# Attention inside a fused layer: one product of queries and keys instead of two, and probabilities turned by DMA

## The chip, the cores and the metric

One Trainium2 chip, one core of it. The metric is the device time of one execution in microseconds (us); three runs of the kernel before gave 1651.43 to 1651.74 us, median 1651.48.

## The reference, cut to what matters

```python
xn = layernorm(x)                                   # x: 1 x 2048 x 512
q = xn @ Wq                                         # 16 heads of 32
k, v = split(xn @ Wkv, 2)                           # 4 key/value heads of 32
scores = q @ k.T / sqrt(32) + tril(idx_s - idx_t) * slope[head]
attn = softmax(where(s <= t, scores, -inf), axis=-1)
x = x + (attn @ v) @ Wo + bo + mlp(xn)              # mlp: 512 -> 4096 -> 512, 4-bit weights, gated GELU
```

The score of query t and key s exists only for s <= t. The kernel needs, for each query, the greatest score (to shift the exponent), the exponentials, their sum and their product with the values.

## The kernel before, in words

Everything has fp32 accuracy: an operand is split in a high and a low fp16 part, and three products (high x high, high x low, low x high) make one. Queries and keys are used as fp32.

The main loop has 16 iterations. Iteration i does head i of the attention and one sixteenth of the MLP (256 of its 4096 columns, all 2048 tokens). It is cut into 48 slots (`SLOTS`, L59). In each slot TensorE issues six MLP matmuls of 512 columns in two halves (`mlp(s, 0)`, `mlp(s, 1)`, L1427 and L1434), and round them the attention's work for that slot: 288 MLP matmuls in an iteration. The order on each engine is written out by the tables of a plan (`FIRST_PLAN` for head 0, `EVEN_PLAN` after it, L126 and L129): which block goes in which slot. Each engine walks the slots by itself, in order, and waits on semaphores.

The attention multiplies queries and keys twice:

- `maximum` (L1318) puts 128 queries on partitions and up to 512 keys in the columns (40 blocks of a head, 17,408 columns). VectorE reduces each block to a maximum (`reduce`, L1622: TENSOR_REDUCE for full blocks, a masked reduction for the 16 on the diagonal, each followed by a read of its accumulator). Four small reductions make a high and a low part of the negated maximum of 512 queries (`negate_max`, L1640), `turn_max` (L1352) turns them on TensorE and ScalarE copies them as two more rows into the query operand (`max_rows`, L1510). This runs about half a head ahead.
- `score` (L1365) puts 128 keys on partitions and up to 512 queries in the columns (36 blocks, 17,408 columns), with the negated maximum added by those two rows. VectorE adds the mask on the diagonal (`causal`, L1613, 16 additions). ScalarE takes exponentials (`exp`, L1493) and rounds them to fp16 (`prob_hi`, L1504); GpSimd makes the low part (`prob_lo`, L1777). Keys already lie on partitions, so the fp16 probabilities are the moving operand of the value products as they are.

`values` (L1391) takes up to 8 blocks at a time, six times a head. Each block gives five products with 32 weight columns, which go to four groups of 32 columns of the array in turn: three value products and two with a column of ones, which make the row sums. `o_copy` (L1518) copies both results, and SyncE's queue gathers them: 12 DMAs of values (`gather_o`, L1218), 8 of row sums, then `load_sums`, the reciprocals (`row_sums`, L273) and their spreading.

SyncE's queue (L1147 to L1273) issues every DMA of the loop in program order, with waits between: queries of the next head in four pieces of four DMAs (`load_q`), keys (`load_k`, each head, two buffers), packed weights, and the six crossbar transposes of the decoded weights (`turn_rows`, L381: high and low rows, 128 x 1024 fp16 each, for three matrices).

## Time and profile before

| | us |
|---|---|
| median of the three runs | 1651.48 |
| the profiled execution: its own time | 1653.03 |
| the profiled execution: its span | 1651.0 |
| one head in the steady part (16 in all) | 92.3 |
| before the main loop / after its last values | about 113 / about 70 |

```profile
PE 1606.0 (97%) x9953; PEld 808.8 (49%) x9953; DVE 1210.7 (73%) x2688; ACT 1059.2 (64%) x1740; POOL 1025.1 (62%) x853
PEclk9989999999999999999999999999999999999999
```

PE is TensorE, PEld its weight loads, DVE VectorE, ACT ScalarE, POOL GpSimd, SPq the queue in which SyncE issues DMAs. The first line has busy time and share of the span; the second the clock granted to TensorE in 40 equal slices, in tenths of full speed. Matmuls are pipelined, so their listed durations overlap; the distance between their starts is what they cost.

### The profile page before, as it was taken

To read this page: it belongs to the slowest core of one execution; us is meant where nothing else is said; L and a number is where in the kernel's file an instruction comes from. 1 tells how busy PE (TensorE), PEld (TensorE's weight loads), DVE (VectorE), ACT (ScalarE), POOL (GpSimd) and SP (SyncE) were. 2 spreads that over 40 slices of the span, in tenths; PEclk is the share of its full clock that TensorE was granted. 3 is DMA by queue.
4 is the path that set the end of the run, shared out by engine and by line. 5 is a ranking of instruction groups with operands and counts; after the bars stand their busy time and mean duration, and the time that the engine had idled before them with its cause. 6 is when DMAs were issued, how large, how long until landed. Compare 5 with 4: busy or idle time off the path is not lost.

```text
span 1651.0 us, 30625 instructions
## 1 busy us (share of the span) xinstructions
PE 1606.0 (97%) x9953; PEld 808.8 (49%) x9953; DVE 1210.7 (73%) x2688; ACT 1059.2 (64%) x1740; POOL 1025.1 (62%) x853
## 2 busy tenths in 40 slices
PE   5979999999999999999999999999999999999998
PEld 4754444444444444444444444454544444444443
DVE  7757877777777777776777777776777777776666
ACT  3326677676767766676767767675767667676650
POOL 3215667576767757576767757576766767575550
PEclk9989999999999999999999999999999999999999
DMA  7872232223122132223222231223132231322135
GB/s 218 226 178 74 43 83 47 70 53 79 31 72 67 45 82 49 70 51 79 38 70 62 48 85 43 74 47 79 43 73 54 53 79 43 77 49 72 43 107 190
DMA packets 203956, 125.75 MB, mean 76 GB/s; under 512 B 156128, under 2 KB 173416, under 8 KB 202104
## 3 DMA queue, kind: packets, MB, share of 16 engines
q1 hardware_dynamic: 199480, 118.16, 29.1%
q10 hardware_dynamic: 4320, 5.64, 1.0%
q8 instruction: 82, 1.34, 0.3%
q14 instruction: 74, 0.61, 0.1%
HBM read 63.31 MB, written 22.42 MB: 52 GB/s over the span
## 4 chain that ended last, share of the span: by engine, by line
PE 84%; DVE 5%; issue 2%; DMA 1%; ACT 1%; POOL 0%; SPq 0%; POOLq 0%; DVEq 0%; ACTq 0%
PE up_ps L1314 20%; PE gate_ps L1314 19%; PE down_ps L1292 18%; PE max_ps L1333 8%; PE o_ps L1385 8%; PE score_ps L1376 4%; PE turn_ps L1376 3%; PE l_ps L1385 2%; DVE prod L1603 1%; DVE acc L1579 1%; PE turn_ps L1361 1%; DVE score_ps L1618 0%; DMA wo_tops<-sc 0%; DVE mxp L1637 0%; DMA l_parts<-lraw 0%
## 5 line engine op out<-in xcount | busy, mean ns | idle before, releaser
L1781 POOL TENSOR_TENSOR plo<-p,phi 128x512 f16<-128x512 f32 (+1 forms) x576 | 664.9, 1160 | 263.1 <-ACT phi L1508 259.0
L1508 ACT ACTIVATE phi<-p 128x512 f16<-128x512 f32 (+1 forms) x576 | 348.7, 605 | 16.3
L1637 DVE TENSOR_REDUCE mxp<-max_ps 128x1 f32<-128x512 f32 x373 | 256.5, 688 | 126.2 <-PE max_ps L1333 125.4
L1789 POOL TENSOR_TENSOR il<-prod,ih 128x512 f16<-128x512 f32 x128 | 156.6, 1223 | 236.1 <-DVE ih L1611 236.1
L1501 ACT ACTIVATE p<-score_ps,pshift 128x512 f32<-128x512 f32 (+1 forms) x321 | 207.9, 648 | 147.4 <-PE score_ps L1376 67.9
L1333 PE MATMUL max_ps<-kst,qst 128*128 128x512 f32 (+2 forms) x610 | 253.9, 416 | 6.7 <-DVE mxp L1637 2.8
L1501 ACT ACTIVATE p<-turn_ps,pshift 128x512 f32<-128x512 f32 (+1 forms) x255 | 170.7, 669 | 105.7 <-DVE turn_ps L1618 55.8
L1633 DVE CUSTOM_DVE_ANT_0 max_ps<-max_ps,mask_row 128x512 f32<-128x512 f32 (+1 forms) x237 | 116.6, 492 | 121.7 <-PE max_ps L1333 120.3
L1314 PE MATMUL gate_ps<-xh,wh 128*128 128x512 f16 x512 | 198.0, 387 | 0.0
L1314 PE MATMUL up_ps<-xh,wh 128*128 128x512 f16 x512 | 197.5, 386 | 0.0
L1292 PE MATMUL down_ps<-wh,ih 128*128 128x512 f16 x506 | 194.9, 385 | 0.0
L1314 PE MATMUL gate_ps<-xh,wl 128*128 128x512 f16 x512 | 194.8, 380 | 0.0
L1314 PE MATMUL gate_ps<-xl,wh 128*128 128x512 f16 x512 | 194.8, 380 | 0.0
L1314 PE MATMUL up_ps<-xh,wl 128*128 128x512 f16 x512 | 194.0, 379 | 0.0
L1314 PE MATMUL up_ps<-xl,wh 128*128 128x512 f16 x512 | 194.0, 379 | 0.0
L1292 PE MATMUL down_ps<-wl,ih 128*128 128x512 f16 x506 | 191.8, 379 | 0.0
L1292 PE MATMUL down_ps<-wh,il 128*128 128x512 f16 x506 | 191.8, 379 | 0.0
L1579 DVE TENSOR_TENSOR acc<-down_ps,acc 128x512 f32<-128x512 f32 x237 | 162.4, 685 | 29.4 <-PE down_ps L1292 25.9
L1376 PE MATMUL score_ps<-qst,kst 128*128 128x512 f32 (+2 forms) x355 | 178.5, 518 | 5.6 <-ACT qst L1516 2.9
L1385 PE MATMUL o_ps<-phi,vst 128*32 128x512 f16 (+3 forms) x1744 | 164.4, 348 | 0.0
L1376 PE MATMUL turn_ps<-qst,kst 128*128 128x512 f32 (+3 forms) x285 | 146.5, 531 | 0.0
L1333 PEld LDWEIGHTS max_ps<-kst,qst 128*128 128x128 f32 x610 | 115.6, 189 | 58.9 <-DVE mxp L1637 20.9
(305 smaller groups left out, 2747.4 us busy)
## 6 DMA issues: line engine op xcount, KB each, us to landing
qst<-q_parts SPq DMA_DIRECT2D x192, 64.0 KB
o<-oraw SPq DMA_DIRECT2D x192, 64.0 KB, 2.0
kst<-k_parts SPq DMA_DIRECT2D x45, 256.0 KB, 4.6
q_parts<-o SPq DMA_DIRECT2D x24, 256.0 KB, 3.3
raw<-L_ffn_gate_W_packed_dram SPq DMA_DIRECT2D x16, 256.0 KB, 3.0
raw<-n_L_ffn_up_W_packed_dram SPq DMA_DIRECT2D x16, 256.0 KB, 3.2
raw<-L_ffn_down_W_packed_dram SPq DMA_DIRECT2D x32, 128.0 KB, 3.4
rb<-l_recips SPq DMA_DIRECT2D x16, 256.0 KB
```

The costliest lines, as they stand in the source:

```text
L1292: mm = nc.tensor.matmul(dst[:], lhs, rhs, start=(q == 0), stop=(q == 5))
L1314: mm = nc.tensor.matmul(dst[:], lhs, rhs, start=(q == 0), stop=(q == 11))
L1333: mm = nc.tensor.matmul(bank[:, 0:cols], qst[:, c, t * P:(t + 1) * P], kst[h % 2][:, m * CH:m * CH + cols], start=True, stop=True)
L1376: mm = nc.tensor.matmul(bank[:, col:col + width], kst[par][:, j * P:(j + 1) * P], qst[:, c, tok:CH], start=True, stop=True, skip_group_che ...
L1385: mm = nc.tensor.matmul(bank[g * HD:(g + 1) * HD, tok:CH], vst[:, j, of * HD:(of + 1) * HD], src[n % PP][:, col:col + CH - tok], start=sta ...
L1501: nc.scalar.activation(p32[n % PR][:, 0:cols], bank[:, 0:cols], ACT.Exp, bias=pshift[:, 0:1]).then_inc(exp_done, 1)
L1508: nc.scalar.activation(phi[n % PP][:, 0:cols], p32[n % PR][:, 0:cols], ACT.Copy).then_inc(phi_done, 1)
L1579: nc.vector.tensor_tensor(acc[:, n % NT, :], bank[:], before, ALU.add).then_inc(acc_done, 1)
L1633: nc.vector.tensor_tensor_reduce(bank[:, 0:cols], bank[:, 0:cols], mask_row[:, CH - cols:CH], 1.0, -3e38, ALU.add, ALU.max, mxp[c % 2][:, ...
L1637: nc.vector.tensor_reduce(mxp[c % 2][:, t, m:m + 1], bank[:, 0:cols], AX.X, ALU.max).then_inc(red_done, 1)
L1781: nc.gpsimd.tensor_tensor(plo[n % PP][:, 0:cols], p32[n % PR][:, 0:cols], phi[n % PP][:, 0:cols], ALU.subtract).then_inc(plo_done, 1)
L1789: nc.gpsimd.tensor_tensor(il[w % 2][:, a, :], prod[a][:], ih[w % 2][:, a, :], ALU.subtract).then_inc(il_done, 1)
```

## The change

Queries and keys are multiplied once, with 128 queries on partitions. VectorE takes each block's maximum as before and then makes the shift of one tile of 128 queries by itself, with queries on partitions, so that ScalarE can take the exponential from the same PSUM block with the shift as its per-partition bias. The scores' second product, the turning of the maxima, the mask additions and the two extra rows go. The PSUM banks become a ring of four for these blocks.

ScalarE's exponential also gives the sum of its row (`accum_out`), one for each of the 40 blocks; the products with ones go, and the gathering of their results. The reciprocals are turned on VectorE in 32 x 32 pieces and stored by four small DMAs.

The probabilities now have queries on partitions, and the value products need keys there. So each part (`PARTS`: a tile of 128 queries and up to 1024 keys; 24 in a head, 136 blocks of 128 x 128) is rounded to fp16 in one ScalarE copy and one GpSimd subtraction, and both results are turned by a crossbar transpose DMA each, issued by SyncE: 48 more in a head. Two buffers for each half (`PH = 2`) stand before the transposes; behind them is a ring of room for 42 blocks. A value product covers 256 queries (two tiles) for one block of keys: 193 products of 256 columns and 24 of 128 in a head, in eight calls.

The work of a head starts six slots before its iteration (`LEAD`), so six slots without MLP work stand ahead of the first one. One plan serves all heads. Keys are loaded every fourth head only, and the order on SyncE's queue is written by slots too.

```diff
+BLOCKS = [(TPC * c + i, m) for c in range(NCH) for i in range(TPC) for m in range(c + 1)]
+PARTS = [(t, a) for t in range(NT) for a in range(t // (2 * TPC) + 1)]
+RING = 42
+LEAD = 6
+TILE_START = tuple(range(4)) + (4, 6, 8, 10) + (12, 16, 19, 23) + (26, 31, 36, 41)
+EXP_LAG = ((1,), (1, 1), (1, 1, 2), (1, 1, 2, 3))
+PART_LAG = ((2,), (2,), (2, 3), (2, 3))
+LOW_LAG, VALUES_LAG = 2, 6
+    for n, (t, m) in enumerate(BLOCKS):
+        last = TILE_START[t] + t // TPC
+        put(tables.block_at, TILE_START[t] + m, n)
+        put(tables.exp_at, last + EXP_LAG[t // TPC][m], n)
+    for p, (t, a) in enumerate(PARTS):
+        at = TILE_START[t] + t // TPC + PART_LAG[t // TPC][a]
+        put(tables.part_at, at, p)
+        put(tables.low_at, at + LOW_LAG, p)
+        if p in LAST_PART:
+            put(tables.values_at, at + VALUES_LAG, t // 2)
...
+LOAD_Q_AT = {2: 0, 9: 1, 21: 2, 40: 3}
+GATHER_AT = {1: 3, 7: 0, 15: 1, 30: 2}
...
+        PR, PH = 3, 2
+        s_ring = (s0_ps, s1_ps, s2_ps, s3_ps)
...
             def _(sp):
+                def turn(h, p, done, rows, dst, turned):
+                    t, a = PARTS[p]
+                    n, count = h * NPART + p, min(t + 1 - 2 * TPC * a, 2 * TPC)
+                    sp.wait_ge(done, n + 1 if done is phi_done else after(n + 1))
...
+                    sp.dma_start_transpose(dst[:, at:at + count, :], rows[n % PH][:, 0:count * P]).then_inc(turned[n % PH], 16)
+                def body(i, par, slots):
+                    for s in slots:
+                        for h, p in items(PLAN.low_at, i, s):
+                            turn(h, p, plo_done, plo, ptl, lo_turned)
+                        for h, p in items(PLAN.part_at, i, s):
+                            turn(h, p, phi_done, phi, pth, hi_turned)
...
             def _(pe):
+                    def block(h, n):
...
+                        if g >= len(s_ring):
+                            pe.wait_ge(exp_done, after(g + 1 - len(s_ring)))
+                        cols = columns(t, m)
+                        nc.tensor.matmul(s_ring[n % len(s_ring)][:, 0:cols], qst[:, c, i4 * P:(i4 + 1) * P],
+                                         kst[:, m * CH:m * CH + cols], start=True, stop=True).then_inc(block_done, 1)
+                    def values(h, u):
...
+                        for n in (last - 1, last):
+                            pe.wait_ge(hi_turned[n % PH], 16 * (n // PH + 1))
+                            pe.wait_ge(lo_turned[n % PH], 16 * (n // PH + 1))
+                        for j in range(2 * u + 2):
+                            both = j <= 2 * u
+                            for src, of in ((pth, 0), (pth, 1), (ptl, 0)):
+                                rows = src[:, at + j:at + j + step + 1:step, :] if both else src[:, at + step + j, :]
+                                todo.append((vst[:, j, of * HD:(of + 1) * HD], rows, 0 if both else P))
...
             def _(act):
+                    def exp(h, n):
...
+                        act.wait_ge(shift_done, h * NT + t + 1)
+                        if p >= PR:
+                            act.wait_ge(plo_done, after(p + 1 - PR))
+                        nc.scalar.activation(p32[p % PR][:, at:at + cols], s_ring[n % len(s_ring)][:, 0:cols], ACT.Exp,
+                                             bias=shift[t % len(shift)][:, 0:1], accum_out=lacc[h % 2][:, t, m:m + 1]
                                              ).then_inc(exp_done, 1)
+                    def part_hi(h, p):
...
+                        if n >= PH:
+                            act.wait_ge(hi_turned[n % PH], 16 * (n // PH))
+                            act.wait_ge(plo_done, after(n + 1 - PH))
+                        nc.scalar.activation(phi[n % PH][:, 0:cols], p32[n % PR][:, 0:cols], ACT.Copy).then_inc(phi_done, 1)
...
             def _(dve):
+                    def negate(h, n):
...
+                        dve.wait_ge(red_done, h * NBLK + n + 1)
+                        if c:
+                            nc.vector.tensor_reduce(top, mxp[t % 2][:, 0:c + 1], AX.X, ALU.max).then_inc(best_done, 1)
+                        nc.vector.tensor_scalar(shift[t % len(shift)][:], top, -1.0, PSHIFT, ALU.mult, ALU.add
+                                                ).then_inc(shift_done, 1)
...
             def _(pool):
+                    def part_lo(h, p):
...
+                        if n >= PH:
+                            pool.wait_ge(lo_turned[n % PH], 16 * (n // PH))
+                        nc.gpsimd.tensor_tensor(plo[n % PH][:, 0:cols], p32[n % PR][:, 0:cols], phi[n % PH][:, 0:cols],
+                                                ALU.subtract).then_inc(plo_done, 1)
```

## Rows read from the trace of the kernel before

**Rows 1.** Windows, two steady heads: length, busy us and instructions, PEclk, DMA share, GB/s

```profile
816.90:909.20 92.30, 92.20 (x591) 45.15 (x595) 68.26 (x155) 63.61 (x105) 62.43 (x52) 1.00 0.26 65
909.20:1001.50 92.30, 92.21 (x592) 45.18 (x593) 68.21 (x155) 63.60 (x105) 62.42 (x52) 1.00 0.26 60
```

**Rows 2.** Chain that ended last, the same value batch of two heads: start, us

```profile
909.23 1.84 PE o_ps L1385 x32
...
1001.55 1.84 PE o_ps L1385 x32
```

**Rows 3.** Timeline of PE: one fp32 block between MLP matmuls: start us, us

```profile
847.99 0.38 PE L1314 MATMUL up_ps<-xl,wh 128*128 128x512 f16 x1
848.02 0.58 PE L1333 MATMUL max_ps<-kst,qst 128*128 128x512 f32 x1
848.45 0.39 PE L1314 MATMUL up_ps<-xh,wh 128*128 128x512 f16 x1
848.67 0.38 PE L1314 MATMUL up_ps<-xh,wl 128*128 128x512 f16 x1
```

**Rows 4.** Timeline of PE: into a value batch and out of it

```profile
841.64 0.38 PE L1314 MATMUL gate_ps<-xl,wh 128*128 128x512 f16 x1
841.95 0.39 PE L1385 MATMUL o_ps<-phi,vst 128*32 128x512 f16 x2
...
843.91 0.38 PE L1385 MATMUL o_ps<-phi,vst 128*32 128x512 f16 x1
844.22 0.39 PE L1314 MATMUL gate_ps<-xh,wh 128*128 128x512 f16 x1
```

**Rows 5.** Timeline of PE: narrow products in the smallest batch

```profile
826.40 0.22 PE L1385 MATMUL o_ps<-phi,vst 128*32 128x128 f16 x2
826.46 0.28 PE L1385 MATMUL o_ps<-phi,vst 128*32 128x256 f16 x2
...
826.56 0.38 PE L1385 MATMUL l_ps<-plo,vst 128*32 128x512 f16 x1
```

**Rows 6.** Groups by form, DVE: busy us, mean ns of one, idle before

```profile
L1618 DVE TENSOR_TENSOR score_ps<-score_ps,mask_st 128x128 f32<-128x128 f32 x151 | 41.2, 293 | 39.9 <-PE score_ps L1376 39.5
L1651 DVE TENSOR_REDUCE mxc<-nmx 128x4 f32<-128x4 f32 x64 | 10.1, 158 | 0.0
L1633 DVE DVE_READ_ACCUMULATOR2_ANT mxp<- 128x1 f32 x256 | 36.1, 141 | 0.0
```

**Rows 7.** Groups by form, ACT and POOL

```profile
L1501 ACT ACTIVATE p<-score_ps,pshift 128x512 f32<-128x512 f32 x272 | 184.8, 679 | 121.9 <-PE score_ps L1376 67.9 <-issue 37.0 <-DVE score_ps L1618 16.2
L1508 ACT ACTIVATE phi<-p 128x512 f16<-128x512 f32 x512 | 322.1, 629 | 14.3
L375 ACT ACTIVATE raw<-wf 128x1024 f16<-128x1024 f32 x48 | 50.5, 1053 | 16.7 <-DVE wf L368 16.6
L1781 POOL TENSOR_TENSOR plo<-p,phi 128x512 f16<-128x512 f32 x512 | 616.3, 1208 | 256.9 <-ACT phi L1508 252.7
L379 POOL TENSOR_TENSOR o<-wf,raw 128x1024 f16<-128x1024 f32 x45 | 98.7, 2193 | 0.0
```

**Rows 8.** Line 385 on SyncE's queue: issue in ns min/median/max, first and last start

```profile
L385 SPq DMA_TRANSPOSE wh<-raw x48: 1232/1268/2557, 97.5 to 1482.8; - x48
```

**Rows 9.** Timeline of SyncE's queue: plain issues back to back

```profile
731.97 1.23 SPq L1161 DMA_DIRECT2D qst<-q_parts  x3
...
734.35 1.79 SPq L1231 DMA_DIRECT2D o<-oraw  x3
736.25 0.61 SPq L292 DMA_DIRECT2D rb<-l_recips  x1
```

**Rows 10.** DMA issues of the page's kind: count, median us from issue to landing

```profile
wh<-raw SPq DMA_TRANSPOSE x48, 3.1
```

**Rows 11.** Windows of 1 us behind the transpose issued at 818.05 us

```profile
819.00:820.00 1.00, 1.00 (x10) 0.60 (x6) 0.00 (x0) 0.00 (x0) 1.00 (x2) 1.00 0.83 145
820.00:821.00 1.00, 1.00 (x7) 0.50 (x6) 0.69 (x3) 0.56 (x2) 1.00 (x2) 1.00 0.60 117
```

More of the change, by code:

```diff
@@ L41 @@
 AUG = 8
-NB = 2
 XS = 2.0 ** 4
@@ L1365, in score @@
-                    def score(n):
-                        c, tiles, _ = BLOCKS[n]
-                        for (ahead, turned), at in plan.turn_after.items():
-                            if at == n and ahead == 0:
-                                pe.wait_ge(brow_done, after(i * NCH + turned + 1))
-                        if n == 0 and i:
-                            pe.wait_ge(brow_done, after(i * NCH + 2))
-                        bank = wait_score_bank(("score", n))
-                        for j, col, tok in tiles:
-                            width = CH - tok
-                            mm = nc.tensor.matmul(bank[:, col:col + width], kst[par][:, j * P:(j + 1) * P],
-                                                  qst[:, c, tok:CH], start=True, stop=True,
-                                                  skip_group_check=True)
-                        mm.then_inc(score_done, 1)
@@ L1673, in body @@
                             inner(n)
-                        if maxima:
-                            negate_max(*maxima[0])
+                        for h, block in blocks:
+                            negate(h, block)
                         if last[0] == "up" and last[3]:
```

773 lines of the change are left out of this document (325 added, 448 removed).

## The prediction

> **What bounds the kernel now.** I read the windows of steady heads first. In a head of 92.3 us TensorE is busy for 92.2 at a granted clock of 1.00 (its upper level, 2.4 GHz), VectorE for 68.3, ScalarE for 63.6 and GpSimd for 62.4, with a DMA share of 0.26 [rows 1]. The chain of waits says the same: it runs through TensorE, and the same value batch comes 92.3 us later in the next head [rows 2]. So TensorE's stream bounds, and the other engines have 24 to 30 us of slack in a head. Since listed matmul durations overlap, I price TensorE by distances between starts. The profiled execution took 1653.0 us, 1.5 above the median of the runs shown; the sum is made against it.
>
> **TensorE, per head.** An MLP matmul is followed by the next after 0.22 us; with one fp32 block of 512 columns between them it takes 0.46 [rows 3], so a block costs 0.245 us. (1) The second product of queries and keys goes: 17,408 columns are 34 such blocks, 8.3 us. (2) Four turnings of maxima go, 2,048 columns at the same price: 1.0 us. (3) Value products. In a big batch 36 products start in the 1.96 us from 841.95 to 843.91, so one of 512 columns costs 0.0545, because four column groups run side by side; entering and leaving the batch costs 0.31 instead of 0.22, twice 0.1 [rows 4]. Before: 5 x 34 + 3 = 173 products of 512, 9.4 us, and six batches, 1.2: 10.6. After: 193 of 256 and 24 of 128 columns are 205 of 256; at half of 0.0545 that is 5.6, and eight batches, 1.6: 7.2. Narrow products keep that pace: after the 128-column ones at 826.40 the 256-column ones start 0.06 later, and the next round 0.10 after these [rows 5]. That saves 3.4. The sum is 12.7 us, so TensorE alone would allow a head of 79.6.
>
> The Trainium skill speaks against (3). "TensorE: Matmul & The Clock Gate", section "Back-to-back issue gap", gives about 81 ns per matmul for streams of weight load and matmul at N=128, however little each computes. By that the 217 products would cost 17.6 us and TensorE would need 90. The trace's column groups start four in about 0.1 us and disagree, but its narrow stretch is short; this is a rival below.
>
> **VectorE.** Sixteen mask additions of 0.293 go (4.7 us), and sixteen small reductions of 0.158 (2.5); 28 small ones come (12 reductions and 16 shifts, 4.4) [rows 6]. 68.3 becomes 65.5, of 80: it still has room, but its slack falls from 24 us to 14.
>
> **ScalarE.** 40 exponentials in place of 36 of the same columns: a copy of 512 columns takes 0.629 and one of 1024 takes 1.053, so the fixed part is 0.2 and four more cost 0.8. Copies to fp16 fall from 36 to 24: -2.4. Four copies of row sums and four of turned maxima go, at 0.6 each: -4.8 [rows 7]. The row sum of each exponential is not in this trace. Its bounds are 0 and, if it is a read like VectorE's accumulator, 0.141 each, twice that if ScalarE is slower: 0 to 11 us; I take the row, 5.6 [rows 6]. 63.6 becomes 62.8. **GpSimd** does the same columns in fewer, wider pieces: 512 take 1.208 and 1024 take 2.193, fixed part 0.22, so 12 fewer save 2.7 and one more addition costs 1.2 [rows 7]: 60.9. Neither bounds, but GpSimd works wholly in the chain copy, subtraction, low transpose, values.
>
> **SyncE's queue**, the resource that the page's first part doesn't list. A 128 x 1024 transpose occupies it for 1.23 to 1.27 us [rows 8], a plain DMA of 32 partitions 0.41 to 0.6, and one that spreads 256 KB 0.61 [rows 9]; about 0.05 lies between two. Unchanged or changed plain work in a head: 16 loads of queries, 6.5 us; 16 gathers of values (12 before, and 8 of row sums go), 10.4; some 12 others (weights, results, four small stores of reciprocals, a quarter of the keys), 6.5; six weight transposes, 7.7. That is 31 us. New are 48 transposes with 272 blocks of 128 x 128. No narrow transpose is in the trace. Lower bound: all by size, 272 x 0.16 = 43.5. Upper bound: all by count, 48 x 1.28 = 61.4. I take a fixed part like a plain DMA's, 0.42, and the rest of the wide one's time by size, 0.1075 a block: 20.2 + 29.2 = 49.4. The queue then needs 80.4 us a head, where TensorE needs 79.6. That is the crux: the change takes 12.7 us from the bound and builds a second bound beside it.
>
> The data behind an issue: two windows after it have DMA shares of 0.83 and 0.60, so 1.4 us of all 16 engines for 256 KB [rows 11]. 34 such amounts are 49 us a head, and 24 were there before [rows 1]: up to 70 of 85. It fits, at longer landings than the 3.1 us of now [rows 10].
>
> "Advanced Engine Details and Errata" of the Trainium skill, section "X-Bar Transpose (TRN2)", says that transposes are as fast as regular DMAs. Were that so of the issue, at 0.61 the queue would need about 62 us and TensorE would bound. The trace disagrees: 1.23 against 0.61 for the same 256 KB.
>
> **What the waits add.** The transposes aren't even over the slots. A slot would be 1.66 us. Slots 1 to 9 hold nine transposes of four to eight blocks, two gathers, two loads of queries and the stores of reciprocals, 19 us of queue in 15; slots 15 to 22 hold nine more, a gather, two weight transposes, weights and queries, 15.5 in 13.3, on top of what is late already. So the queue is 4 to 5 us late twice a head. Values come four slots (6.6 us) after the low transpose's slot; of that the landing takes 3.1, which leaves 3.5. I expect TensorE to wait 1 to 1.5 us in each burst, and longer when landings stretch: 3 us. GpSimd and ScalarE wait too, since only two buffers stand before the transposes, and behind them in order stand the MLP's low product and the gate's square. A second wait: in the last four tiles the next tile's first block needs the bank of the fourth block before it, whose exponential is planned one slot earlier, behind the maximum, the shift and ScalarE's gate work. Three times 0.5 us. In all 4.5 to 5 us on top of 80: a head of 85.
>
> **Start and end.** Six slots without MLP stand ahead, six blocks of 0.25 on TensorE at least, each at most with 0.7 of maximum and 0.7 of exponential in series: 1.5 to 10, I take 4. At the end the reciprocals are ready earlier and one addition comes on: -1. Together +3, with ±5.
>
> **The sum.** 16 x (92.3 - 85.0) = 116.8, less 3: 1653.0 - 113.8 = 1539; 1.5 lower for the median: 1538.
>
> **Rivals.**
> A, TensorE stays the bound. Narrow transposes are issued by size (queue 74.5 us) and the lags cover the landings. For it: TensorE was busy for 92.2 of 92.3 although the plan was tight. Against: every engine now has a third less slack. Head 79.6: 16 x 12.7 - 3 = 200, 1451.
> B, slower than before. The issue of a transpose costs the same however narrow it is, and the queue needs 31 + 61.4 = 92.4 us, plus some 2.5 for the waits at which nothing behind may go: 95. 16 x 2.7 + 3 more, 1698. It decides from a mean of 1.22 us an issue with its gap, (92.3 - 2.5 - 31) / 48; the forecast has 1.03. For it: the six transposes measured take 1.232 at least and nearly always, and the issue is over before the first data moves, so it isn't a matter of bandwidth. Against: plain DMAs vary by shape, 0.41 to 0.61 [rows 9].
> C, value products are paced by count and not by columns: 217 at the 0.0545 of the wide ones [rows 4], 11.8 instead of 5.6. TensorE needs 85.8, a head 88: 1587. The narrow starts speak against it [rows 5]. By the figure of the Trainium skill's page named above, 0.081, a head would be 90 and the time about 1620, as an estimate.
> D, the handshakes between VectorE and ScalarE bound: the row sum costs twice the row (68 us on ScalarE), and each tile waits at its bank. Head 88 to 91: about 1600.
> That the change doesn't take the second product away is excluded by its code.
>
> **Chances.** Forecast (head 82 to 88) 0.45, A 0.2, B 0.24, C 0.03, D 0.08. A measurement here can tell 0.2% (3.3 us) from no change. Faster: the forecast, A, C and D, 0.76, less 0.03 where D meets a slow queue and the head reaches 92: 0.73. Same 0.02. Slower 0.25. The range goes from A to B with their uncertainty of start and end: 1448 to 1698. The faster cases alone span 1448 to 1615.
>
> **What would show it.** Right: value products of 256 columns four in 0.11 us; score blocks still 0.245; a narrow transpose's issue near 0.5 us; SyncE's queue busy for over 90% of a head, and TensorE idle some 5 us a head before the value products (waiting for DMA landings) and before first blocks of the last tiles. Wrong: no idle time on TensorE (A); all transposes at 1.23 us and long waits of ScalarE and GpSimd for landings (B); value products evenly 0.08 apart (C); TensorE waiting for exponentials in most slots (D).

## The result, and the profile after

The changed kernel takes 1849.34 us (median of 4 runs, 1844.45 to 1854.23), the kernel before 1651.45 on the same chip (1650.84 to 1651.74): a ratio of 1.120, 95% interval 1.116 to 1.124. It was forecast 7% faster, with 1698 us as the upper end, and it is 12% slower.

The page of the changed kernel: busy time and share of each engine, TensorE's granted clock in 40 slices, and the first queue's share of the 16 DMA engines.

```profile
span 1843.7 us, 29952 instructions
PE 1495.3 (81%) x9281; PEld 718.2 (39%) x9281; DVE 1262.5 (68%) x2642; ACT 996.4 (54%) x2124; POOL 996.7 (54%) x670
PEclk9978989999899999999989999899988999998889
q1 hardware_dynamic: 789176, 253.53, 72.6%
SPq 11%; DMA 10%; PE 6%; POOL 3%; issue 3%; ACT 2%; DVE 1%; ACTq 0%; POOLq 0%; DVEq 0%
```

No engine is full. The chain that ended last, in the last line, can be followed for 36% of the span only; in that part it names SyncE's queue and the DMA first, where the chain before went through TensorE [rows 2]. Windows of three steady heads, the counterpart of [rows 1]:

```profile
953.80:1057.00 103.20, 86.08 (x547) 39.17 (x547) 73.38 (x152) 59.39 (x129) 60.73 (x40) 0.93 0.74 136
1057.00:1159.30 102.30, 83.80 (x547) 39.13 (x547) 71.01 (x152) 59.96 (x129) 60.38 (x41) 0.95 0.77 136
1159.30:1261.30 102.00, 85.39 (x546) 39.40 (x545) 72.00 (x152) 58.30 (x126) 60.76 (x40) 0.93 0.74 135
```

A head is the distance between the first gate matmuls of two heads. After the first, which takes 109.5, the next fourteen have a mean of 103.5 us, between 100.9 and 106.5. TensorE is idle for some 18 us of it and its granted clock has fallen from 1.00 to 0.93-0.95.

Where the 311 us of the miss lie: 16 x (103.5 - 85.0) = 296 in the heads. Outside the heads' steady pace, 1843.7 - 16 x 103.5 = 187.7 us stand against 174.2 before (1651.0 - 16 x 92.3): 13.5 more, where 3 were put. The last 5 us are the profiled run's distance to the median (1845.56 against 1849.34), the 1.5 us that the forecast took off for the median of before, and rounding.

The transposes of the probabilities on SyncE's queue: duration in ns min/median/max. These are the answer to [rows 8].

```profile
L1167 SPq DMA_TRANSPOSE pth<-phi x384: 1174/1252/5238, 122.9 to 1777.9; - x192
L1167 SPq DMA_TRANSPOSE ptl<-plo x384: 1160/1252/3384, 126.2 to 1783.0; - x192
```

They have one to eight blocks. Sorted by width, from the same records (ns; the high halves have the same minima within 20, and the medians of the last line):

```
blocks       1     2     3     4     5     6     7     8
low, min   1160  1178  1183  1198  1201  1228  1220  1232
median     1222  1236  1205  1284  1281  1296  1310  1254
high, med  1932  1232  1271  1216  1275  1287  1300  1252
```

**The issue of a transpose takes 1.2 us whether it moves one block or eight.** Some take longer (the mean of all is 1.34), but not the wide ones in particular: the longest median is that of the high halves with one block. A stretch of the queue's own timeline (start, duration of all, count) shows what that makes of a head:

```profile
1108.12 1.18 SPq L1167 DMA_TRANSPOSE ptl<-plo  x1
1109.40 1.24 SPq L1167 DMA_TRANSPOSE pth<-phi  x1
1110.69 0.48 SPq L1143 DMA_DIRECT2D qst<-aug_rows  x1
1111.22 1.23 SPq L1145 DMA_DIRECT2D qst<-q_parts  x3
1112.49 1.20 SPq L1167 DMA_TRANSPOSE pth<-phi  x1
1113.79 3.29 SPq L1167 DMA_TRANSPOSE ptl<-plo  x2
1117.17 2.60 SPq L1167 DMA_TRANSPOSE pth<-phi  x2
1119.88 1.26 SPq L384 DMA_TRANSPOSE wh<-raw  x1
1121.18 1.35 SPq L384 DMA_TRANSPOSE wl<-o  x1
1122.62 2.60 SPq L1167 DMA_TRANSPOSE ptl<-plo  x2
```

Between two issues there is a gap of 0.04 to 0.10 us, seldom more. In the head from 1057.0 to 1159.3 the queue's 98 issues sum to 96.4 us (49 transposes of probabilities 66.1, a mean of 1.35, the 49 others 30.3); that leaves 5.9 us, 0.06 for each gap, and the queue is full. Over the fourteen heads the mean is 64.2 us for 48 transposes, 31.7 for 50 others, 6.3 for gaps, and only 1.3 of waiting. No transpose is issued before its half is ready, so no waiting hides inside an issue, and half of the high halves have been ready for 3.2 us or more when their issue starts, half of the low ones for 2.6. What waits for the queue, over the whole span (us in total, times, longest):

```profile
POOL plo L1703 <- DMA ptl<-plo: 566.5, 209, 12.8
PE o_ps L1355 <- DMA ptl<-plo: 150.5, 72, 8.5
ACT gl L1417 <- PE gate_ps L1313: 139.0, 70, 5.8
ACT p L1436 <- DVE shift L1572: 132.1, 97, 5.7
```

GpSimd waits 35 us a head for its halves to be turned, then TensorE for the same, and then the MLP's steps for TensorE.

### The profile page after: what moved, and what is told of

Its sections match the earlier page's. It is cut to its first block and busy times, and to the rows that moved or that the text cites. A ratio compares the mean times of both kernels' runs of the same rounds, so it can differ in the third digit from the quotient of the medians.

```text
span 1843.7 us, 29952 instructions
## 1 busy us (share of the span) xinstructions
PE 1495.3 (81%) x9281; PEld 718.2 (39%) x9281; DVE 1262.5 (68%) x2642; ACT 996.4 (54%) x2124; POOL 996.7 (54%) x670
## 3 DMA queue, kind: packets, MB, share of 16 engines
q8 instruction: 75, 1.23, 0.3%
## 5 line engine op out<-in xcount | busy, mean ns | idle before, releaser
L1703 POOL TENSOR_TENSOR plo<-p,phi 128x1024 f16<-128x1024 f32 (+7 forms) x384 | 614.6, 1608 | 639.7 <-DMA ptl<-plo 566.5
L1436 ACT ACTIVATE p<-s_ps,shift 128x512 f32<-128x512 f32 (+3 forms) x640 | 393.1, 619 | 226.0 <-DVE shift L1572 132.1
L1448 ACT ACTIVATE phi<-p 128x1024 f16<-128x1024 f32 (+7 forms) x384 | 308.7, 807 | 273.9 <-issue 186.8
L1330 PE MATMUL s_ps<-kst,qst 128*128 128x512 f32 (+3 forms) x640 | 360.6, 565 | 86.8 <-ACT p L1436 68.9
L1551 DVE TENSOR_REDUCE mxp<-s_ps 128x1 f32<-128x512 f32 x384 | 260.5, 682 | 144.1 <-PE s_ps L1330 143.4
L1355 PE MATMUL o_ps<-pth,vst 128*32 128x256 f16 (+1 forms) x2304 | 142.2, 313 | 204.2 <-DMA ptl<-plo 150.5
L1553 DVE CUSTOM_DVE_ANT_0 s_ps<-s_ps,mask_row 128x128 f32<-128x128 f32 (+3 forms) x256 | 126.3, 493 | 138.3 <-PE s_ps L1330 137.7
L1355 PEld LDWEIGHTS o_ps<-pth,vst 128*32 128x32 f16 x2304 | 99.4, 109 | 267.5 <-issue 201.2
L1330 PEld LDWEIGHTS s_ps<-kst,qst 128*128 128x128 f32 x640 | 129.0, 202 | 190.6 <-ACT p L1436 74.7
L1355 PE MATMUL o_ps<-ptl,vst 128*32 128x256 f16 (+1 forms) x1152 | 145.7, 315 | 0.0
```

The source lines that it names most:

```text
L1330: nc.tensor.matmul(s_ring[n % len(s_ring)][:, 0:cols], qst[:, c, i4 * P:(i4 + 1) * P], kst[:, m * CH:m * CH + cols], start=True, stop=True ...
L1355: mm = nc.tensor.matmul(dst if tok else dst.rearrange("p (a n) -> p a n", a=2), lhs, rhs, start=k < VPARTS, stop=k + VPARTS >= len(todo), ...
L1436: nc.scalar.activation(p32[p % PR][:, at:at + cols], s_ring[n % len(s_ring)][:, 0:cols], ACT.Exp, bias=shift[t % len(shift)][:, 0:1], accu ...
L1448: nc.scalar.activation(phi[n % PH][:, 0:cols], p32[n % PR][:, 0:cols], ACT.Copy).then_inc(phi_done, 1)
L1551: nc.vector.tensor_reduce(mxp[t % 2][:, m:m + 1], bank[:, 0:cols], AX.X, ALU.max).then_inc(red_done, 1)
L1553: nc.vector.tensor_tensor_reduce(bank[:, 0:cols], bank[:, 0:cols], mask_row[:, CH - cols:CH], 1.0, -3e38, ALU.add, ALU.max, mxp[t % 2][:, ...
```

## The experiments

Three theories came out of this. **Q**: SyncE's queue is full of issues of fixed length. **R**: the data of the transposes, or their landing, bounds, and the issues are only stretched. **B**: the two buffers ahead of the transposes bound. The last part adds a fourth. Each kernel is the changed one with the edit shown (of a diff only the lines that matter, not always adjacent), a head is the mean from the second on, and times stand beside 1651.2 to 1653.2 for the kernel before on the same chips. Where no number of runs is given there was one; four runs of the changed kernel lie 0.5% apart, so a difference of that size says nothing.

**Fewer issues: no low transposes.** The value products of the low halves read zeros, set once.

```diff
-    for h, p in items(PLAN.low_at, i, s):
-        turn(h, p, plo_done, plo, ptl, lo_turned)
-    pe.wait_ge(lo_turned[n % PH], 16 * (n // PH + 1))
-    if n >= PH:
-        pool.wait_ge(lo_turned[n % PH], 16 * (n // PH))
```

> The changed kernel without the 24 low transposes of a head (the low half of the probabilities is left out of what the value products see: its buffer is set to zero once, and the products with it still run). Theory Q (SyncE's queue is full of issues of fixed length): the queue's 102 us a head lose 24 x 1.35 = 32, so TensorE bounds again at about 80 plus a few us of waits: head 81 to 86, time 1480 to 1560. Theory R (the data, or its landing, bounds): half of the transposed data goes too, so a gain of the same sign; the run only sets the size against the next one. Theory B (two buffers and their round trip bound): the high halves still go round two buffers, head 90 to 100, time 1650 to 1800.

1637.42 us, head 90.5, the queue's issues 59 us of a head. 24 issues and their landings are worth 212 us, but more was expected: TensorE isn't back at 80, and its clock is 0.96. Something besides the queue holds the head at 90.

**Same count, less data.** Every transpose moves one block of 128 x 128; the rest of the ring is zeros.

```diff
-    sp.dma_start_transpose(dst[:, at:at + count, :], rows[n % PH][:, 0:count * P]).then_inc(turned[n % PH], 16)
+    sp.dma_start_transpose(dst[:, at:at + 1, :], rows[n % PH][:, 0:P]).then_inc(turned[n % PH], 16)
```

> All 48 transposes of a head are still issued, at the same places, but each moves one block of 128 columns (the rest of the turned probabilities is left out: zeros set once). Transposed data falls from 34 units of 256 KB to 6 a head. Q: the count stays and an issue stays at 1.18 us or more against a mean of 1.37: the queue needs 93 to 98 us, time 1700 to 1800, at most 8% under the changed kernel. R: the DMA share falls to half and landings from 3.2 to 2.3 us: head 82 to 88, time 1500 to 1600. B: round trips become 1 us shorter of 8: about 1650.

1771.5 us, head 98.8. The issues, by the transposes' own row:

```profile
L1167 SPq DMA_TRANSPOSE pth<-phi x384: 1093/1177/3114, 124.2 to 1706.7; - x192
L1167 SPq DMA_TRANSPOSE ptl<-plo x384: 1093/1182/2387, 127.3 to 1711.4; - x192
```

48 of 272 blocks are left, the DMA share falls from 0.74-0.77 to 0.33, and the head by 5 us only. The issue costs 1.18 us in the median. The queue is still full: its issues and gaps take 97 us of the 98.8. R falls as the bound of this kernel; what the data does is to stretch the mean issue, 1.22 us here and 1.34 with all of it.

**More buffers**: three of halves, two of probabilities.

```diff
-        PR, PH = 3, 2
+        PR, PH = 2, 3
```

> Three buffers instead of two ahead of each kind of transpose, paid for with two instead of three buffers of fp32 probabilities. Nothing left out. Q: no change, 1810 to 1880. B: ScalarE's and GpSimd's copies no longer wait for a landing two parts back: head 88 to 93, time 1610 to 1690. R: no change.

1855.03 us, head 104: no change, and the queue is as full as before (2 us of waiting in a head). B falls. The edit pays with a buffer of probabilities, so it doesn't tell what three of each would do.

**Half as many issues of twice the width.** High and low halves stand side by side in one buffer, and one transpose of up to 2048 columns turns both (two probability buffers, three of halves).

```diff
-    sp.dma_start_transpose(dst[:, at:at + count, :], rows[n % PH][:, 0:count * P]).then_inc(turned[n % PH], 16)
+    at = 2 * ROOM[t] + 4 * TPC * a
+    sp.dma_start_transpose(pt[:, at:at + 2 * count, :], both[n % PH][:, 0:2 * count * P]).then_inc(turned[n % PH], 16)
```

> High and low part of each part of the probabilities lie side by side in one buffer and are turned by one transpose of up to 2048 columns: 24 issues a head instead of 48 for the same bytes; three such buffers, two of fp32 probabilities. Q with a flat issue (1.2 to 1.4 us also at 2048 columns): the queue needs 69 us, TensorE bounds, head 80 to 86, time 1460 to 1560, faster than both kernels. Q with an issue that grows past 1024 columns (2.5 us): 24 x 2 = 48 plus 37, head 88 to 92, time 1600 to 1660. R: bytes and landings are as before or worse, head 95 to 103, time 1720 to 1850.

1738.1 us (4 runs, 1735.96 to 1744.96), ratio to the kernel before 1.053, interval 1.050 to 1.056. All of the data and the whole computation are there, so merging is worth 111 us. But the time is far above both ranges that Q gave and lies in R's. The head is 96.7, with 80 us of issues and 11 of waiting on the queue, so something besides the queue holds it. The issue is no longer flat:

```profile
L1164 SPq DMA_TRANSPOSE pt<-both x384: 1170/1769/5671, 124.9 to 1674.7; - x192
```

With two blocks its median is 1.20, with 16 it is 1.97 (minimum 1.53, mean 2.55), and the DMA share is 0.79.

**Other work off the queue**: 28 plain DMAs of a head (16 loads of queries, 12 gathers of values) are issued from ScalarE's program on its own queue, once with the 48 transposes and once with the merged ones.

```diff
-    gather_o(h, c)
-    load_q(i + 1, LOAD_Q_AT[s])
+    if 0 <= i and GATHER_AT.get(s):
+        gather_o(act, i - (c == NCH - 1), c)
+    if 0 <= i < LAST and s in LOAD_Q_AT:
+        load_q(act, i + 1, LOAD_Q_AT[s])
```

> The changed kernel with 28 plain DMAs of a head moved from SyncE's queue to ScalarE's: the 16 loads of the next head's queries and 12 of the 16 gathers of values (those of tokens 0 to 511 stay). All 48 transposes stay as they are. Theory Q (SyncE's queue is full of issues of fixed length): the queue loses 28 issues, 14.2 us with 1.7 of gaps, so 102 becomes 86, and the head falls from 103 to 90-92, where the kernel without low transposes already stood: 1640 to 1680 us. ScalarE pays 14 us and stays below 80. Theory R (what bounds is the transposes' data or landing, and the issues are only stretched to fill the time): the issues stretch further and the head stays at 100 or more: 1800 to 1850.

> The merged version (high and low halves side by side, one transpose of up to 2048 columns for both, 24 a head, two probability buffers and three of halves) with the 28 plain DMAs of a head on ScalarE's queue as well. The merged version stood at 1738 us, head 96, with 79.6 us of issues on SyncE's queue. Theory Q: the queue, at 82 per cent of the head, still sets the late transposes; with 64 us it does not, head 90, 1640 to 1680. Theory R (in the merged version the data of the transposes or their landing bounds, the queue no longer): 1715 to 1745, no change beyond 1 per cent.

1762.29 us for the first (called the relieved kernel below), head 97.4, issues for 165 of 200 us, so 80 in a head. The sign and half the size of what Q said: when 16 us of issues go, 6 come off the head, and something else takes over at 97. The queue now waits for 10 us a head. ScalarE's program spends 15 us a head on the issues that it took over, and what these cost there isn't separated. The second took 1752.6 (4 runs, 1746.48 to 1755.83), ratio 1.061, interval 1.059 to 1.063: nothing gained over the merged version, rather 0.8% lost. There the queue is not the bound: its issues are 68 us of a head, and it waits for 27.

**The merged version with little data**: 24 issues of one block.

```diff
-    sp.dma_start_transpose(pt[:, at:at + 2 * count, :], both[n % PH][:, 0:2 * count * P]).then_inc(turned[n % PH], 16)
+    sp.dma_start_transpose(pt[:, at:at + 1, :], both[n % PH][:, 0:P]).then_inc(turned[n % PH], 16)
```

> The merged version with every one of the 24 transposes cut to one block of 128 x 128, so that only 24 of 544 blocks of data move in a head; the value products read mostly zeros. Same count of issues as in the merged version. Theory R (data or landing bounds the merged version): head falls from 96 to about 90 or less, 1580 to 1650. Theory Q' (the count of issues and the two probability buffers bound it): 1715 to 1745.

(The expectation says 544 blocks; it is 272, both halves counted.) 1643.37 us, head 91, DMA share 0.27. So the merged version pays 95 us for its data. With the data the issues also shorten, from 81 us a head to 59; as the relief of the queue gained nothing, it is the data and its landing that I take for the bound, but the two aren't separated by a run.

**What is left without any transpose.** Neither half is turned, the value products read zeros after waiting for their last low half.

```diff
-    for h, p in items(PLAN.part_at, i, s):
-        turn(h, p, phi_done, phi, pth, hi_turned)
-    pe.wait_ge(hi_turned[n % PH], 16 * (n // PH + 1))
+    pe.wait_ge(plo_done, after(last + 1))
```

> The changed kernel without any probability transpose: neither the high nor the low halves are turned, and the value products read zeros, set once, after waiting for the low half of their last part. Everything else computes. Nothing is left of the new load on SyncE's queue or of landings. Theory C (a second limit of about 90 us a head lies in the handshakes of TensorE, VectorE, ScalarE and GpSimd alone): as without low transposes, head 88 to 91, 1600 to 1640. Theory L (the second limit is the remaining round trip of the transposes: buffers that come free only with the landing): TensorE bounds again at the 79.6 us that the prediction worked out for it, head 80 to 83, 1460 to 1510.

1616.66 us, head 90.8. With the whole new load on the queue gone, the change gains 35 us and not 200. Its window, and VectorE's groups over the whole span:

```profile
900.00:1100.00 200.00, 179.97 (x1183) 82.60 (x1175) 161.79 (x326) 129.29 (x280) 134.97 (x88) 0.97 0.22 54
```

```profile
L367 DVE TENSOR_TENSOR wf<-dec,sc 128x512 f32<-128x512 f16 x96 | 99.2, 1036 | 0.1
L358 DVE TENSOR_SCALAR dec<-dec 128x1024 int32<-128x1024 int32 x48 | 62.0, 1292 | 0.1
L354 DVE TENSOR_SCALAR dec<-raw 128x512 int32<-128x512 int32 x48 | 47.0, 979 | 0.0
L351 DVE TENSOR_SCALAR dec<-raw 128x512 int32<-128x512 int32 x48 | 36.4, 758 | 0.0
L1609 DVE COPY cur<-tab 128x6 f32<-128x6 f32 x15 | 27.1, 1806 | 0.0
```

The same groups of the kernel before, four over its span and, in a fence of its own, the copy in one of its heads:

```profile
L368 DVE TENSOR_TENSOR wf<-dec,sc 128x512 f32<-128x512 f16 x96 | 83.1, 869 | 0.1
L359 DVE TENSOR_SCALAR dec<-dec 128x1024 int32<-128x1024 int32 x48 | 41.8, 870 | 0.1
L355 DVE TENSOR_SCALAR dec<-raw 128x512 int32<-128x512 int32 x48 | 22.3, 465 | 0.0
L352 DVE TENSOR_SCALAR dec<-raw 128x512 int32<-128x512 int32 x48 | 22.7, 474 | 0.0
```

```profile
L1696 DVE COPY cur<-tab 128x6 f32<-128x6 f32 x1 | 0.2, 166 | 0.0
```

Unchanged instructions take up to twice as long, and a copy of six columns 1.81 us in place of 0.17. That is about as long as one of the new wide subtractions on GpSimd (2.16 us for 1024 columns). VectorE's reduction of a score block, which reads PSUM, took 0.684 here and 0.688 before. This gave a fourth theory. **P**: while a wide GpSimd subtraction runs, VectorE's work inside SBUF stands still. The trace of this kernel shows it directly:

```profile
950.73 2.14 POOL L1697 TENSOR_TENSOR plo<-p,phi 128x1024 f16<-128x1024 f32 x1
950.93 0.15 DVE L1566 TENSOR_SCALAR shift<-mxt 128x1 f32<-128x1 f32 x1
951.04 1.86 DVE L1609 COPY cur<-tab 128x6 f32<-128x6 f32 x1
```

All 15 copies of the loop start inside a subtraction and end 26 to 32 ns after it. The casts, the three unpacking steps and the product `wf` behave alike: not one of them ends while a GpSimd instruction that covers its start is still at work. Not all work inside SBUF stands still, though: the shifts of one column run in 0.15 us in the middle of a subtraction, as the second line shows, and reductions from PSUM run there at their old length.

That the lengthening costs time is another matter. **H**, against it: the handshake of reduction, shift, exponential and the next block's bank binds by itself. Five kernels on top of the one without transposes. The first cuts the subtractions to 128 columns; the second takes the wait for the shift away, by a fixed bias and scale; the third does both:

```diff
-    nc.gpsimd.tensor_tensor(plo[n % PH][:, 0:cols], p32[n % PR][:, 0:cols], phi[n % PH][:, 0:cols],
+    nc.gpsimd.tensor_tensor(plo[n % PH][:, 0:P], p32[n % PR][:, 0:P], phi[n % PH][:, 0:P],
```

> The kernel without any probability transpose (1617 us, head 90.5), and GpSimd's 24 low subtractions of a head cut to 128 columns each (0.43 us in place of up to 2.2). The rest computes. In that kernel VectorE was busy for 73.4 us a head against the 65.5 of the prediction, because its unpacking steps took 0.94 to 1.3 us in place of 0.43 to 0.81 and the small copy of the scales 1.86 in place of 0.17. Theory P (VectorE's instructions wait for GpSimd's wide subtractions, and that slows the whole chain): VectorE falls to 66-68 us a head, the head to 84-87, 1530 to 1575 us. Theory H (the handshake reduction, shift, exponential, bank of the next block binds by itself, whatever GpSimd does): VectorE's instructions get shorter but the head stays at 89 to 91, 1595 to 1620.

```diff
-    act.wait_ge(shift_done, h * NT + t + 1)
+    act.wait_ge(red_done, h * NBLK + n + 1)
...
-    bias=shift[t % len(shift)][:, 0:1]
+    bias=fixed[:], scale=0.001
...
+    pe.wait_ge(red_done, after(g + 1 - len(s_ring)))
```

> The kernel without any probability transpose, and its exponentials take a fixed bias and a scale of 0.001, so that they wait for their own block's reduction in place of the tile's shift; a block of scores waits for its bank's reduction as well as for its exponential. All maxima, shifts and subtractions are still computed, in the same order on each engine. Theory H: the wait of ScalarE for the shift (12 us a head) goes and TensorE gets its banks back earlier; head 82 to 86, 1495 to 1560 us. Theory P (what is lost is lost to VectorE's slowed instructions and to the order of the MLP's steps, not to the shift): 1590 to 1620.

> The last two edits together in the kernel without any probability transpose: low subtractions of 128 columns, and exponentials that do not wait for the tile's shift. Whatever binds beside them remains. If these two handshakes are the whole second limit, TensorE bounds at its 79.6 us: head 80 to 82, 1455 to 1500 us. If a third one is there (the order of the MLP's steps on VectorE and ScalarE, or the two-piece ring of banks), head 84 to 88, 1530 to 1590.

The last two keep all the work and split the subtractions, at 512 columns and, with 256 in the place of `CH`, at 256:

```diff
-    nc.gpsimd.tensor_tensor(plo[n % PH][:, 0:cols], p32[n % PR][:, 0:cols], phi[n % PH][:, 0:cols],
+    for k in range(0, cols, CH):
+        low = nc.gpsimd.tensor_tensor(plo[n % PH][:, k:min(k + CH, cols)], p32[n % PR][:, k:min(k + CH, cols)],
```

> The kernel without any probability transpose, and GpSimd's low subtractions wider than 512 columns are made as two instructions of at most 512 (1.2 us each in place of 2.2). Same work, GpSimd pays 14 times 0.22 = 3 us more a head. Theory P: an instruction of VectorE that waits for GpSimd waits at most 1.2 us in place of 2.2, so the copy of the scales falls below 1.3 us, VectorE's busy time by 2 to 3 us a head, and the head by 1 to 2: 1580 to 1605 us. Theory H, or an order of waits in which VectorE waits as often but shorter: no change in time, 1610 to 1630.

> The kernel without any probability transpose, with GpSimd's low subtractions in pieces of at most 256 columns: all the work, shorter instructions, and 7 to 10 us a head more on GpSimd than with wide ones, some 72 in all. Theory P1 (what counts is how long one GpSimd instruction holds VectorE up): below the 86 us of the split at 512, head 82 to 84, 1490 to 1525 us. Theory P2 (what counts is how much of the time GpSimd is at work): VectorE waits as much in all and GpSimd's subtractions end later, head 86 to 89, 1545 to 1600.

```
without transposes               time us   head   VectorE's copy of 6 columns
wide subtractions (up to 1024)   1616.7    90.8   1.81
pieces of at most 512            1547.5    86.0   0.97
pieces of at most 256            1522.8    84.2   0.22
128 columns in all               1458.6    80.1   0.17
wide, no wait for the shift      1589.4    89.0   1.82
128 in all, no wait for shift    1449.5    79.4   0.17
```

Windows from 900 to 1100 us, in the order of pieces of 512, of 256, 128 in all, and 128 without the wait for the shift:

```profile
900.00:1100.00 200.00, 187.23 (x1272) 87.05 (x1270) 166.59 (x358) 138.67 (x303) 150.89 (x131) 1.00 0.23 56
```

```profile
900.00:1100.00 200.00, 187.18 (x1265) 87.21 (x1263) 168.10 (x356) 139.11 (x301) 167.96 (x207) 1.00 0.24 59
```

```profile
900.00:1100.00 200.00, 196.55 (x1377) 92.83 (x1378) 158.21 (x379) 146.59 (x326) 80.66 (x101) 1.00 0.28 65
```

```profile
900.00:1100.00 200.00, 198.40 (x1388) 93.61 (x1387) 160.32 (x382) 146.65 (x327) 80.42 (x102) 1.00 0.29 67
```

The copy's column is its mean over the loop, and it depends on what the copy meets: in the kernel before no GpSimd instruction runs beside any of the 16 copies. With pieces of 512 all 15 end with the piece that they meet. With pieces of 256, 14 of them meet only the last 0.15 us of another instruction, and the one that meets a piece takes 0.71.

P holds. The kernel with 128 columns in all, at 1458.6, gained even more than P's 1530 to 1575. Splitting the subtractions adds work to GpSimd (61 us a head, then 65, then 71) and yet takes 69 and then another 25 us off the time, so it is the length of one instruction that counts, or where the split lets VectorE in, and not how much GpSimd has to do. VectorE's busy time falls less than I had put for the pieces of 512 (73.4 a head to 71.6, and 70.8 with 256; it waits more often, but shorter), while the head gains more than the 1 to 2 us put: what matters is how late a single step of the handshake can get. From 84 to 80 the last kernel leaves work out as well as length, so that step isn't separated. H is small: 27 us with wide subtractions, 9 with small ones, the latter hardly more than two runs of one kernel can differ. With both gone the head is 79.4 us at a clock of 1.00.

The Trainium skill has this on its page "SBUF — State Buffer", section "Who interferes with whom": VectorE's copies, casts and tensor-scalar operations in a two-port mode, and any VectorE instruction with two inputs in SBUF, share a port pair with GpSimd that is locked for a whole instruction. The trace agrees on which groups grow: the copy, the three unpacking steps, the cast (0.54 before, 0.80 in the changed kernel), and the product `wf` of two SBUF inputs (0.87 before, 1.04 without transposes), but not the reduction from PSUM.

**Back in the full kernel.** The same splits with all transposes in place, four kernels: the changed kernel with pieces of 512; the merged one with the 28 plain DMAs moved, with 512 and with 256; the relieved one with 256.

> The changed kernel as it is, with its 48 transposes a head, and only GpSimd's low subtractions split into instructions of at most 512 columns; without transposes this edit took 69 us away. Theory Q (with all transposes in place SyncE's queue sets the head alone, 98 issues that need 102 us with their gaps, and the slowed VectorE hides behind it): 1830 to 1850 us, head 103, VectorE 2 us a head shorter. Theory S (the limits add: what VectorE loses makes transposes late that the queue can't catch up): 1770 to 1800.

> The merged version with the 28 plain DMAs on ScalarE's queue (1753 us, head 97, queue 67 us of issues, DMA engines busy for 0.82), and low subtractions of at most 512 columns. Theory D (the transposes' data bounds it: 0.213 us of all 16 engines for each of 272 blocks, 58 us, with the rest 79 of 97, and landings of up to 11 us): no more than 1 per cent faster, 1735 to 1755. Theory S (late data and slowed VectorE add up in the chain): 4 to 5 us a head faster, as without transposes, 1670 to 1700.

> The same with low subtractions of at most 256 columns (0.67 us each; GpSimd pays 10 us a head more than with 1024 wide ones and comes to 72). Theory D: as with 512, 1735 to 1755. Theory S: VectorE waits at most 0.7 us, and the head is another 1 to 2 us shorter than with 512 unless GpSimd's own 72 us make the low parts late: 1650 to 1690.

> The unmerged kernel with the 28 plain DMAs on ScalarE's queue (1762 us, head 98, queue 85 us of issues of 98), and low subtractions of at most 256 columns. Theory Q (the queue at 87 per cent still sets the late transposes): 1740 to 1765. Theory S: VectorE's lost 7 us come back, head 92 to 94, 1670 to 1710.

1847.3, 1743.8, 1755.9 and 1767.5 us: none moves by more than 0.6%, up or down. The first says that the full queue sets the changed kernel's 103.5, and the limit at 90 is hidden behind it. The others, at heads of 97 to 98, are also held by something above that limit.

**The relieved kernel with little data**: pieces of 512 and one block in each of the 48 transposes.

```diff
-    sp.dma_start_transpose(dst[:, at:at + count, :], rows[n % PH][:, 0:count * P]).then_inc(turned[n % PH], 16)
+    sp.dma_start_transpose(dst[:, at:at + 1, :], rows[n % PH][:, 0:P]).then_inc(turned[n % PH], 16)
```

> The unmerged kernel with the 28 plain DMAs on ScalarE's queue, low subtractions of at most 512 columns, and each of the 48 transposes cut to one block of 128 x 128, so that 48 of 272 blocks move; the value products read mostly zeros. All 70 issues stay on SyncE's queue, about 75 us of them. Theory D (the transposes' data and late landings set the 98 us of the relieved kernel): the compute chain's limit with split subtractions is next, head 86 to 88, 1545 to 1590 us. Theory Q (the queue's issues, with the waits before which nothing behind may go, still set it): head 94 or more, 1690 to 1765.

1688.4 us, head 92.9: just below what Q gave and well above the 86 to 88 of the theory that data and landings set the pace. The queue is busy for 82% of the time. Of the 16.6 us a head in which it isn't, 5 are gaps between issues and some 11 are waits, nearly all before transposes, many of them for a half that isn't made yet.

So of the 97.4 us of the relieved kernel 4.5 are data (97.4 to 92.9; splitting alone, at 256, changed nothing there), and 7 more, down to the 86.0 without transposes, come with the issues and their fixed order: a queue that waits for one half holds back all that stand behind it. That is argued, not shown; how this part divides between issue time, order and buffers stays open.

No version of the change with all of its work beats the kernel before: the best, merged, stands 5% above it.

## Why the prediction was wrong

**The step that failed** is the price of a narrow transpose on SyncE's queue: "I take a fixed part like a plain DMA's, 0.42, and the rest of the wide one's time by size, 0.1075 a block". The price is nearly flat: 1.16 us at least for one block and 1.23 for eight, so 0.01 a block on top of 1.15. Of the two bounds the upper one was true, and it wasn't high enough either, because the data stretches issues: 48 cost 67.3 us with their gaps where 61.4 was the bound, and 49.4 was taken. The other 50 came to 31.7 us, 34.9 with their gaps, against the 31 worked out with theirs. So the queue needs 67.3 + 34.9 = 102.2 us a head, where 80.4 was put, and with 1.3 of waiting the head is 103.5.

**A second step** failed behind it, and would have undone the forecast by itself: that a head without a slow queue is 80 us and a few of waits. The same plan without any transpose takes 90.8, for the reason under VectorE below. With no transposes to pay for at all the change gains 35 us, so neither the forecast's 85.0 nor rival A's 79.6 could have come.

**Rival B** had the right mechanism and the right sign. Its own condition, a mean above 1.22 us an issue with its gap, was met with 1.40. Its price was 95 where 103.5 was measured, since it took 1.28 an issue with the gap (48 x 0.12 = 6 us) and 4 too few for the other issues, and so its 1698 was the end of the range and the time lay outside. I gave it 0.24 because plain DMAs vary from 0.41 to 0.61 [rows 9]; that is no evidence on transposes. Nor could [rows 8] decide: its transposes all have one width. The sign of the forecast hung on a price that no row had. B's remark that the issue is over before the first data moves is nearly so (in the kernel before the data starts 1.18 us after the issue's start, in the median, 0.06 before its end), but bandwidth does enter: with the data of all blocks the mean issue is 1.34 instead of 1.22.

**TensorE** was right. With the other limits gone the head is 79.4 at a clock of 1.00, against 79.6. The changed kernel shows 85.1 us of busy time a head at a mean clock of 0.94, and 85.1 x 0.94 is 80.0, as a rough estimate. Value products keep the pace of the columns (start and duration, kernel with small subtractions): four start in 0.11 us.

```profile
944.55 0.27 PE L1350 MATMUL o_ps<-ptl,vst 128*32 128x256 f16 x1
944.55 0.28 PE L1350 MATMUL o_ps<-pth,vst 128*32 128x256 f16 x2
944.65 0.27 PE L1350 MATMUL o_ps<-ptl,vst 128*32 128x256 f16 x1
944.66 0.28 PE L1350 MATMUL o_ps<-pth,vst 128*32 128x256 f16 x2
```

Rival C falls here: these column groups start one product per 0.027 us. So does, for them, the figure of 81 ns for a matmul at N=128 that I set beside it from the Trainium skill, "TensorE: Matmul & The Clock Gate", section "Back-to-back issue gap". My sums by that figure were also off: it gives TensorE 91.6 us, not 90, and so about 1643 us, not 1620.

**VectorE** was put at 65.5 and took 72.1 (mean of the three windows). The counts and durations of what was removed and added were right; that GpSimd's wider instructions make VectorE's unchanged ones longer was not in the sum. I had entered the wider pieces as a pure saving of 2.7 us. In the changed kernel it hides behind the queue; without transposes, shorter pieces alone, with all the work, bring the head from 90.8 to 84.2. **ScalarE**: 62.8 forecast, 59.2 measured. The row sum is a read of 0.199 us where 0.141 was taken, but the listed durations overlap here too: after an exponential with a read the next instruction starts 0.085 us later than it does without one. So 40 reads take some 3.4 us a head, where 5.6 was put; the rest of the difference isn't sorted out. **GpSimd**: 60.9 forecast, 60.6 measured.

**The data behind the issues**: up to 70 us of all 16 engines in a head were forecast (the two terms, 49 and 24, make 73), and 0.75 x 102.5 = 77 came. The landing has kept its median, 3.2 against 3.1 [rows 10], with a longest of 10.1. I had written "it fits". In the changed kernel it does; the merged one loses 95 us with it.

**The waits.** A wait of 4.5 to 5 us a head was added to the larger of two bounds. In the changed kernel the larger bound, the queue, waits for 1.3, and TensorE idles for 18 because it follows the queue. Rival D's handshakes, put at 88 to 91 us for another reason, are close to the 90.8 of the kernel without transposes, but the row sum costs 3.4 us of ScalarE's time and not 11, and the waits for the shift explain 27 of that kernel's 167 us above the one with neither handshake.

**The clock.** Nothing in the sum asked what TensorE's clock does when the engine idles. It stood at 1.00 in all steady heads before; here it is 0.93 to 0.95 with some 18 us of idle time a head, 0.97 in the kernel without transposes, and 1.00 again in the windows of the kernels whose heads are 86 us or less. It shows in the value products, which follow a wait: 31% of the wide ones start 0.053 us apart in the changed kernel, the pace of the lower level (1.2 GHz), and none do without transposes. I take this for a result of the waits and not their cause: the queue is full whatever TensorE's pace. No run sets the clock by itself.

## What to carry to other kernels

Count the issues on each DMA queue, and price a crossbar transpose by count, not by size: here the hold was fixed per transpose up to eight blocks of 128 x 128, and what is saved on the bound engine is worth nothing once the queue's sum passes it. Where GpSimd runs beside VectorE, ask how long one GpSimd instruction is, not only how long all of them are; a wider piece saves GpSimd's fixed part and may cost the engine beside it far more. In a trace, look for instructions that didn't change and take longer than before. And when rows of before bound a price from both sides with a factor of 1.4 between the ends, and the two ends fall on different sides of zero, a value between them that is borrowed from another kind of operation is no evidence for the sign: both ends then deserve about the same chance.

## What the runs showed of the hardware beyond expectation

- An issue of a crossbar transpose on SyncE's queue takes 1.16 to 1.23 us at least from 128 to 1024 columns (1.09 at least for 128 where little other data moves); at 2048 columns 1.53 at least, with a median of 1.97 when the DMA engines are 0.79 busy. With one block in each, the median landing is 2.4 us from the issue's start, with the usual mix 3.2.
- 272 blocks of 128 x 128 take some 58 us of all 16 DMA engines (a share of 0.77 of 102.3 us with them, 0.22 of 90.8 without), 0.21 us each, as an estimate from these shares.
- A copy of six columns on VectorE takes 0.17 us alone. If it starts inside a subtraction on GpSimd it ends 26 to 33 ns after that: it took 1.86 us in the median with 1024 columns and 1.02 with 512, and 0.71 the one time that it met a piece of 256.
- ScalarE's `accum_out` adds a read of 0.199 us behind each exponential, which overlaps with both neighbours and delays the next instruction by 0.085 us.
